# A graph layer's edge features and destination rows, loaded for two steps per transfer

## The reference

```python
h = jnp.maximum(_layernorm(x, axis=-1), 0.0)
x_i = h[dst]; x_j = h[src]
tmp = jnp.concatenate([x_i, x_j, edge_attr], axis=1)
r = jax.nn.relu(tmp @ W1 + b1)          # W1: 128 x 128
msg = r @ W2 + b2                       # W2: 128 x 48
out = x + jax.ops.segment_sum(msg, dst, num_segments=12500)
```

## Time and profile before

| What | Value |
|---|---|
| Median of 3 runs | 4880.79 us (4862.08 to 4881.68) |
| Span of the profiled execution | 4876.7 us |
| PE (matmul) busy | 3666.9 us, 75% |
| GpSimd busy | 2754.5 us, 56% |
| VectorE busy | 2327.4 us, 48% |
| ScalarE busy | 1681.4 us, 34% |
| SyncE's DMA queue | 217,238 packets, 195.30 MB |
| GpSimd's DMA queue | 92,864 packets, 187.75 MB |

### The profile page before, as it was taken

How to read it: one execution, slowest core, us unless ns; L and a number is a source line. 1 busy time by engine, 2 the same in 40 slices (tenths; PEclk the granted TensorE clock), 3 DMA queues, 4 the chain that set the end, 5 groups by cost and what they waited for, 6 DMA issues and landing times. The chain is left out here.

```text
span 4876.7 us, 87591 instructions
## 1 busy us (share of the span) xinstructions
PE 3666.9 (75%) x18452; PEld 3372.7 (69%) x18452; DVE 2327.4 (48%) x6092; ACT 1681.4 (34%) x6025; POOL 2754.5 (56%) x2916
## 2 busy tenths in 40 slices
PE   4676777777788777777788777777777777777776
PEld 4676667676777776766677667676777667677766
DVE  4644444444445444444444444444444444444443
ACT  3333333333333333333333333333333333333332
POOL 5455555555555555555555555555555555555555
PEclk9877786777777777777776777777776777777765
DMA  5522222222223322222222222222222222222223
GB/s 171 117 77 75 72 77 73 74 75 73 75 73 80 77 75 78 73 77 74 76 75 75 75 76 74 78 76 74 77 74 78 74 75 75 77 73 77 76 75 83
DMA packets 310441, 384.87 MB, mean 79 GB/s; under 512 B 98900, under 2 KB 250261, under 8 KB 309238
## 3 DMA queue, kind: packets, MB, share of 16 engines
q0 software_dynamic: 92864, 187.75, 15.2%
q1 hardware_dynamic: 217238, 195.30, 14.1%
q10 hardware_dynamic: 208, 0.57, 0.1%
HBM read 366.25 MB, written 16.97 MB: 79 GB/s over the span
## 5 line engine op out<-in xcount | busy, mean ns | idle before, releaser
L543 POOL DMA_INDIRECT gath<-b_table,idx x2838 | 2686.0, 946 | 2087.9 <-ACT idx L647 1221.9
L1285 PEld LDWEIGHTS ps<-rhs,lhs 96*128 96x128 f32 x5676 | 1078.1, 262 | 545.9 <-issue 380.9
L1285 PE MATMUL ps<-rhs,lhs 96*128 96x128 f32 x5676 | 1121.2, 352 | 439.9 <-issue 226.2
L1293 PE MATMUL ps<-onehot,gath 128*128 128x48 f32 x5676 | 1007.1, 327 | 559.6 <-ACT gath L663 554.6
L1293 PEld LDWEIGHTS ps<-onehot,gath 128*128 128x128 f32 x5676 | 982.5, 255 | 620.4 <-ACT gath L663 614.3
L1310 PE MATMUL ps<-h_tab,p_hot 128*128 128x480 f32 (+1 forms) x4104 | 1396.4, 480 | 0.0
L1310 PEld LDWEIGHTS ps<-h_tab,p_hot 128*128 128x128 f32 x4104 | 937.1, 251 | 62.8
L647 ACT COPY idx<-src_sb 128x3 int32 (+1 forms) x942 | 184.3, 196 | 2244.4 <-remote 1671.7
L984 DVE TENSOR_TENSOR onehot<-ps,dst_rel 128x144 f32<-128x144 f32 x946 | 288.7, 305 | 1182.3 <-remote 907.8
L1021 DVE TENSOR_TENSOR nodes<-ps,nodes 48x48 f32 x946 | 189.2, 200 | 914.0 <-remote 405.5
L684 ACT ACTIVATE work<-ps,work 128x80 f32<-128x80 f32 x2508 | 614.3, 393 | 0.0
(11 more groups left out here) (127 smaller groups left out, 1341.6 us busy)
## 6 DMA issues: line engine op xcount, KB each, us to landing
nodes<-dst_row SPq DMA_DIRECT2D x946, 72.0 KB
lhs<-in_edge_t SPq DMA_DIRECT2D x946, 48.0 KB
gath<-b_table,idx POOLq DMA_INDIRECT x2838
rhs<-a_table SPq DMA_DIRECT2D x946, 24.0 KB
work<-key_row SPq DMA_DIRECT2D x57, 256.0 KB
nodes<-dst_row SPq DMA_DIRECT2D x73, 96.0 KB
work<-in_edge_t SPq DMA_DIRECT2D x146, 32.0 KB
b_table<-nodes SPq DMA_DIRECT2D x7, 512.0 KB
```

What stands on the lines that cost most here:

```text
L543: pool.indirect_dma_start(gath[:, u, t, :], None, b_table, bass.IndirectOffsetOnAxis(ap=idx[:, u, t:t + 1], axis=0)).then_inc(gathered[u], 16)
L1285: mm = nc.tensor.matmul(ps_z[:, k % 2, t * P:(t + 1) * P], lhs[:, u, t * P:(t + 1) * P], rhs[:, u, :], start=True, stop=True)
L1293: mm = nc.tensor.matmul(ps_sum[:, k % FOLD * WIN:(k % FOLD + 1) * WIN], gath[:, u, t, :], onehot[:, u, t, :], start=(t == 0), stop=(t == s ...
```

## The change

`load_edges` is replaced by `load_edge_pair`. It is called for even k alone and loads the destination numbers of steps k and k + 1 in one transfer (768 numbers into 48 partitions, the two slots' places lying side by side) and their features in another (32 partitions, two pieces of 384 each, one per slot). Both report to one semaphore per pair of slots. Since it overwrites two slots, it waits for z of step k - 3 instead of k - 4. `load_a` stays one transfer per step; both are issued behind the pair's transfers in the even iteration. What else the iteration issues (`load_tail`, `load_key`) stands behind both. `make_hot_t` waits for the pair's semaphore and for its own step's row of `a_table`.

```diff
@@ -89,6 +89,7 @@
     assert BLOCKS * PARTS >= node_tiles and RUN_PARTS[0] * words <= BANK and 2 * runs == PERIOD
     assert sum(RUN_BLOCKS) == BLOCKS
     assert PERIOD == 4 * SLOTS and LEAD == SLOTS and early_tiles == EARLY_A + EARLY_B + EARLY_C
+    assert STEP_TILES[0] == STEP_TILES[1] and ROUND == 2
     assert rounds * gen_cols * gen_k == n_nodes and front_piece * pieces == front
 
     a_table = nc.dram_tensor("a_table", [padded, hidden], F32).ap()
@@ -164,6 +165,7 @@
         slot_cols = [STEP_TILES[u % ROUND] * P for u in range(SLOTS)]
         slot_at = [win_at + sum(slot_cols[0:u]) for u in range(SLOTS)]
         dst_bc = [nodes[e_row:e_row + WIN, slot_at[u]:slot_at[u] + slot_cols[u]] for u in range(SLOTS)]
+        dst_bc_pair = [nodes[e_row:e_row + WIN, slot_at[u]:slot_at[u] + 2 * slot_cols[u]] for u in range(0, SLOTS, 2)]
         first_at = win_at + sum(slot_cols)
         first_node = nodes[e_row:e_row + WIN, first_at:first_at + groups]
         bc_at = first_at + groups
@@ -254,7 +256,7 @@
         idx_ready, hot_ready, hott_ready = sem("idx_ready"), sem("hot_ready"), sem("hott_ready")
         gathered = [sem(f"gathered{u}") for u in range(SLOTS)]
         loaded = [sem(f"loaded{u}") for u in range(SLOTS)]
-        dst_loaded = [sem(f"dst_loaded{u}") for u in range(SLOTS)]
+        edges_loaded = [sem(f"edges_loaded{b}") for b in range(SLOTS // ROUND)]
         z_ready, z_added, r_ready = sem("z_ready"), sem("z_added"), sem("r_ready")
         summed, sums_copied, b2_ready = sem("summed"), sem("sums_copied"), sem("b2_ready")
         folded, out_added = sem("folded"), sem("out_added")
@@ -370,14 +372,16 @@
             sp.dma_start(w2_sb, w2).then_inc(w2_in, 16)
             sp.dma_start(b2_bc, b2.partition_broadcast(P)).then_inc(w2_in, 16)
 
-            def load_edges(k, it, first):
+            def load_edge_pair(k, it, first):
                 s, u = it * PERIOD + k, k % SLOTS
                 if not first:
-                    sp.wait_ge(z_ready, s - SLOTS + 1)
+                    sp.wait_ge(z_ready, s - SLOTS + 2)
                 cols = step_tiles(k) * P
-                sp.dma_start(dst_bc[u], dst_flat[:, ds(tile_of(k, it) * P, cols)].partition_broadcast(WIN)
-                             ).then_inc(dst_loaded[u], 16)
-                sp.dma_start(lhs[e_row:k_rows, u, 0:cols], edge_t[:, ds(tile_of(k, it) * P, cols)]).then_inc(loaded[u], 16)
+                sp.dma_start(dst_bc_pair[u // 2], dst_flat[:, ds(tile_of(k, it) * P, 2 * cols)].partition_broadcast(WIN)
+                             ).then_inc(edges_loaded[u // 2], 16)
+                sp.dma_start(lhs[e_row:k_rows, u:u + 2, 0:cols],
+                             edge_t[:, ds(tile_of(k, it) * P, 2 * cols)].rearrange("p (s c) -> p s c", s=2)
+                             ).then_inc(edges_loaded[u // 2], 16)
 
             def load_key(c, it, first=False):
                 n = c + it
@@ -407,8 +411,8 @@
                     sp.dma_start(key_row, key_sb[:, 2, 0:p_cols]).then_inc(key_stored, 16)
                     sp.wait_ge(dst_row_stored, 16)
                     sp.wait_ge(ones_ready, 3)
-                    for k in range(SLOTS):
-                        load_edges(k, 0, True)
+                    for k in range(0, SLOTS, 2):
+                        load_edge_pair(k, 0, True)
                 if c == 6:
                     sp.wait_ge(key_stored, 16)
                     sp.wait_ge(words_kept, 1)
@@ -444,9 +448,10 @@
             def cycle(c, it, first=False, final=False, more=True):
                 for j in range(PERIOD + EXTRA if final else PERIOD):
                     k = LEAD + c * PERIOD + j
-                    if k >= SLOTS:
-                        load_edges(k, it, False)
+                    if k >= SLOTS and k % 2 == 0:
+                        load_edge_pair(k, it, False)
                         load_a(k, it)
+                        load_a(k + 1, it)
                     if final and 0 <= j - 7 - EXTRA < pieces:
                         store_front(j - 7 - EXTRA)
                     if j == 0 and 0 < c <= EARLY:
@@ -988,8 +993,8 @@
 
             def make_hot_t(k, it):
                 s, g, u = it * PERIOD + k, group_of(k, it), k % SLOTS
-                dve.wait_ge(dst_loaded[u], 16 * fills(k, it))
-                dve.wait_ge(loaded[u], 32 * fills(k, it))
+                dve.wait_ge(edges_loaded[u // 2], 32 * fills(k, it))
+                dve.wait_ge(loaded[u], 16 * fills(k, it))
                 if k >= SLOTS:
                     dve.wait_ge(z_ready, s - SLOTS + 1)
                     dve.wait_ge(b2_ready, s - SLOTS + 1)
```

## The result

| | before | after |
|---|---|---|
| median of the runs | 4881.24 us (4862.08 to 4887.42, 4 runs) | 5008.52 us (4992.51 to 5014.87, 4 runs) |
| profiled execution, span | 4876.7 us | 5005.0 us |
| early cycles 1 to 16, sum | 1323.9 us | 1452.2 us |
| late cycles 17 to 56, sum | 3159.6 us | 3144.7 us |

What follows compares the result with a forecast made beforehand. GpSimd's gathers were taken as nearest to the bound, not alone: GpSimd also waits for ScalarE's index copy. Terms 10 + 71.5 + 12.5 + 24 = 118 us on 4876.7, plus 4.1, gave 4999 us; range 4800 to 5120.

Steps and rivals of the forecast that it cites:

- Second-kind tails: 16 tails loaded at j = 6: 11 cost 6.5 us each (71.5), 5 only an added row, 2.5 each (12.5).
- First-kind tails: 16 early tails loaded at j = 0: only the added row counts, 1.5 us each, 24 us.
- Early cycles in all: Cycles 1 to 16: the costs of both tail kinds, 84 + 24 = 108 us; each cycle 6 to 7 us longer.
- Later gate of ordinary pairs: Pairs wait for z of k - 3, not k - 4: 10 us lost, ends 0 and 45.
- load_key: At j = 14, behind one more row load and a later wait; its user comes three steps later: 0.
- The low end of the sum: Least slowdown from adding the parts' low ends: 52.5 us, which gives 4933 us.
- part 2: Transfer pieces twice as long, 1536-byte runs turned to 3072: taken as 0, between -10 and +10 us.
- signs named for the profile after: L1095's counterpart waits 190 to 300 us; early cycles 6 to 7 us longer; j = 6 pair's first transfer follows the burst.
- Rival (a): Tails come no later, as SyncE has fewer instructions in each slow stretch: 4881 us, chance 0.14.
- Rival (b): Faster: SyncE's transfers feed the slow stretch, fewer shorten it, GpSimd waits 204 or 407 us less; about 4795 or 4474; chance 0.17.
- Rival (c): Much slower: the later gate stalls the pairs everywhere, 2.5 us in each of 263, 660 us: 5540 us, chance 0.06.

Runs made afterwards that it cites:

- e3: Kernel before, with only SyncE's wait in iterations j = 0 and j = 6 of cycles 1 to 16 one step later (z of k - 3): 4969.04 us, ratio 1.016.
- e1: The change, with the a_table row of step k + 1 issued behind the tail instead of ahead; later gate kept: 4958.87 us, ratio 1.0135.
- e2: The change, with load_tail written ahead of the pair's wait in the same iteration: 4845.99 us, ratio 0.9907.
- e11: The change with tail loads earlier (j = 10 a cycle ahead, j = 4), on a chip where the kernel before took 4782.80: 4739.57 us, ratio 0.9923.
- e9: The change unedited, run again beside the kernel before (4863.79 us): 5000.27 us, ratio 1.0265.
- e4: Kernel before, without loads of destination numbers and edge features after the first four steps: 4797.29 us, ratio 0.9825.
- e10: Kernel before, without any of SyncE's three step loads after the first four steps, on a slow chip: 4751.47 us in one run beside 4863.79.
- e12: Kernel before (single loads) with tail loads earlier (j = 10 a cycle ahead, j = 4), on a slow chip: 4752.94 us, ratio 0.9937.
- e7: Kernel before (single loads) with tail loads earlier (j = 10 a cycle ahead, j = 4), on the quick chip: 3663.55 us, ratio 0.9998.
- e8: Kernel before (single loads) with load_tail ahead of load_edges at j = 0 and j = 6, on the quick chip: 3661.31 us, ratio 0.9994.

## Why the prediction was right, and where its terms were off

4999 us was forecast and 5008.52 came. The mechanism is shown: the change puts the tails' loads behind a later gate and one more row. The gate alone has its price (e3), the row has one on top of it (the change less e1), and both taken away (e2, e11) take the loss away. VectorE's idle time before the 32 early tails (from the trace, start of L1100 less the end of what ran before), with the early cycles:

| | first kind, us | second kind, us | cycles 1 to 16, us |
|---|---|---|---|
| before | 48.0 | 99.5 | 1323.9 |
| after | 95.7 | 188.5 | 1452.2 |
| e9, the change again | 100.4 | 198.5 | 1462.0 |
| e3, gate alone | 83.1 | 168.7 | 1403.8 |
| e1, gate without the row | 67.1 | 149.3 | 1405.7 |
| e2, tail ahead | 6.3 | 33.3 | 1287.5 |

Term by term:

- **Second-kind tails**, forecast 71.5 + 12.5 = 84 us: idle time rose by 89.0. The size fits. The forecast had the gate open in the burst, quick rows and a slow tail. In 11 of the 16 the gate opened so. In the other 5, the one of the rows above among them, it opened on z itself within a run; there the rows were slow and the tail quick.
- **First-kind tails**, forecast 24 us: 47.7, about 3.0 each and not 1.5. The failing step is "z of k - 3 arrives in the same burst as that of k - 4, so only the added row counts". With the gate alone (e3) these 16 already lose 35.1. The trace before could have told: in 6 of the 16, z of k - 3 ended after SyncE had passed the gate. And the one tail of the earlier trace rows was taken for all 16. The loss lies in the eight unlike it, which hardly waited before (2.0 us together): 47.9 with the change, 48.3 in e9, 38.0 in e3. The other eight had 46.0 and have 47.8, 52.1 and 45.1.
- **Early cycles in all**, forecast 84 + 24 = 108 us, or 6.75 a cycle: 128.3, or 8.0. The new idle time before the tails is 136.7 us. The two need not go together: e3 has 104.3 us of it and cycles 79.9 us longer, e1 68.9 and 81.8.
- **Later gate of ordinary pairs**, forecast +10: the 40 late cycles were 14.9 us shorter, in e9 18.4, and in e1 and e2 12.5 and 12.1 shorter than in e3 on their own chip. The sign was wrong. Rows that were reckoned late were not: L1002 waits 1.1 us for them. That SyncE comes to the gate with a shorter queue would explain it and is not shown. e4 shows what two transfers fewer a step give, 20.3 us; one fewer fits between. No run takes this gain apart further.
- **load_key**, forecast 0: L1037 waits 105.2 us for it where it waited for nothing, 73.8 of it in late cycles. Yet those cycles are no longer: VectorE's idle time whose end the profile puts down to "remote" fell there from 337.8 (L1021) to 164.0 us before L1026 and rose from 645.9 to 779.4 before L989. So the wait seems to stand in place of another; no run takes it away alone. The 0 held for the time and not for the wait.
- **What is left**: 128.3 - 14.9 = 113.4 of the span's 128.3. 12.3 lie ahead of cycle 0, which begins at 180.5 instead of 168.2. That start lies between 161.6 and 183.1 in the profiles of e1 to e4, e9, e10 and e12, and at 128.9 in e11. e3 has the front part of the kernel before unchanged and begins cycle 0 at 178.9, so such a shift comes without the change.

So the closeness of the sum owes something to luck: the tails cost 20 us more than forecast and the late cycles 25 less, and the front, which had no term, gave 12. The low end of the sum also left out the -10 of part 2; with it, it is 4923.

Of the signs named for the profile after, the row of L1100 for rhs_p shows 174.6 us, under the 190 to 300; only with the 109.6 us put down to "issue" is it 284.2. The early cycles grew by 8.0 us each, not 6 to 7. The pair of j = 6 followed the burst in 11 of 16.

**Rival (a)**, the tails come no later: refuted by the rows above. **Rival (b)**, a slow stretch fed by SyncE's transfers: refuted on chips of the first sort at any size near its 204 or 407 us. Without a step's features and destinations GpSimd waits 1199.5 us (e4), without any of the three loads 1080.5 (e10), and the copy starts a median 1.65 and 1.56 us after the sixth gather's end, 1.69 before. The Trainium skill (DMA: Bandwidth & Descriptors, "Rules for kernel authors") advises to coalesce small transfers, those under 64 KB above all. Of the two merged here only the features' (48 KB) lay under that. The change lost 2.5%: what may come of the rule here is at most the 0.3 to 0.5 us a late cycle, and on the quick chip pairs lose 0.4%. The Trainium skill's other rule there, to issue a transfer early and wait late, e11 and e12 bear out on a slow chip (0.8% and 0.6%); on the quick one e7 gained nothing. **Rival (c)** needed L1002 to wait more than 50 us for loads, and it waits 1.1 in the cycles and 8.4 in all; in e2, where it does wait 81.2 us for its rows, the kernel is still faster than before.

**Open:** what makes the slow stretch. It goes with the chip or its condition: in the kernel before, 874 of 7000 of SyncE's register instructions took over 450 ns; in e8, 0 of 7038 did, with the same SyncE program but for the tails' place. The change itself was not run on the quick chip, nor e8's order on a slow one.

## What to carry to other kernels

A merged transfer waits for the later of its parts' gates, and everything behind it in the queue waits as well: look for what else that queue issues there, not only at the merged loads. Here a third fewer issues for the steps, beside the bound, gave 0.4% or less in the late cycles, and a tail one gate and one row later cost 2.6% of the span (128.3 of 4876.7 us). A load that is used just after it lands should be moved ahead first (j = 6 to j = 4, and j = 0 to j = 10 of the cycle before: 0.6 to 0.8% here); after that, whether transfers are merged hardly mattered. And before a price worked out on one shown place is multiplied by their number, look whether the others wait too: of the 16 early tails of the first kind, the eight that did not are the ones that paid.

## What was not expected of the hardware

The same program takes 3664 us on one chip and 4783 to 4890 on others, and on one of these 4890 and 4783 in two sets of runs. On the quick chip the mean granted clock was 0.866 (e8) for 0.746 before, GpSimd's gathers follow each other 0.30 us apart, and the wait that stands out is that for the gathered data (L1006 waits 805.5 us for it, e8). On the others ScalarE's copy, which waits for matmuls, starts a median 1.5 to 1.7 us after the sixth gather's end (1.69 before, 1.65 in e4, 1.56 in e10), even with SyncE's step loads gone. Ratios from one chip do not carry over to the other: early tails gave 0.6% on one and nothing on the other.
